# Moving the second half's combine behind the last expert, and the first w1 loads onto the ScalarE queue, in an eight-core recurrent + MoE layer

## Chip, cores and metric

The kernel runs on the 8 cores of one Trainium2 chip. Each core works on one of 8 sequences (2048 tokens of width 1024) and exchanges nothing with the others. The metric is the device time in microseconds of the slowest core.

## The reference, cut to what matters

```python
xn = _layernorm(x)
s  = _L0_attn_ref(xn, ...)               # recurrent attention
g  = _silu(_L0_ffn_ref(xn, ...))         # 8 routed experts + 1 shared
return x + s * g
# _L0_ffn_ref:
gates = sum(one_hot(top_k(softmax(x @ w_router.T), 2)) * vals)
acc = gelu(x @ Ws1.T + bs1) @ Ws2.T + bs2
acc = acc + sum_e gates_e * (gelu(x @ W1_e.T + b1_e) @ W2_e.T + b2_e)
return SCALE * acc
```

Every expert is computed for every token and weighted by its gate, which is zero for the experts that are not chosen.

## The kernel before

The program is recorded in Python as one list of instructions for each engine; each engine runs its list in order. The helper `op` derives semaphore waits from the last writer and the readers of whole tiles, so a read of one block of `acc` waits for the last write to any block of it. An engine's list holds its DMA issues too, and these wait in place: what stands behind a waiting DMA issue waits as well.

Stages, in order: the prologue normalises and transposes x; A and B compute the recurrent part; B2 computes `s` and writes it to DRAM as `s_scr` in 16 blocks of 128 tokens. Meanwhile GpSimd's queue casts all expert weights to bf16 copies in DRAM (`w1s`, `w2s`). A barrier ends each stage. The last stage, `ph_ffn`, is the subject here.

`ph_ffn` first loads router weights and biases (L861 to L866), then computes the gates of 16 token blocks, one after the other (L874 matmuls, L884 Exp on ScalarE, a chain of small VectorE operations, L914 transpose). Then it treats the tokens in two halves (`th` = 0, 1) of 1024. For each half it sets `acc` to the gated output biases (L970, L974) and goes through 9 experts. Of each expert:

- phase 1 (L995): 512 matmuls of 128x128 by 128x512 make the hidden layer, with `w1s` coming in four 2 MB quarters into two buffers `w1b`; ScalarE applies Gelu (L1006). The first two quarters of the next expert are loaded ahead by ScalarE's queue (L1043); only the very first expert's are loaded at L984, quarter 0 by SyncE and quarter 1 by GpSimd, as quarters 2 and 3 are.
- phase 2 (L1027), in two parts `qq` of four token blocks: 256 matmuls each, with `w2s` in 256 KB pieces through a ring of six buffers, loaded alternately by SyncE and GpSimd (L1017). After each part VectorE adds the eight banks of PSUM to `acc` (L1053, or L1059 for the shared expert, which is the last of the nine).

Then the *combine*: for each of the half's 8 token blocks, load x and s, ScalarE's Tanh of `acc`, four VectorE operations, and the store of `out`. There is one `gfin` tile, and two each of `xres` and `sres`. For the first half this stands behind its last expert, with the DMAs on SyncE (L1075 to L1093): loads of a block, then its store, then the loads of the next. For the second half `mk_combine_t1` makes eight pieces of work with all DMAs on ScalarE's queue (L935 to L958); four are put into the list during part `qq` = 1 of the last expert, behind its matmul steps 4, 12, 20 and 28, and the other four are put behind everything. They may start early because blocks 0 to 3 of `acc` are final after part `qq` = 0.

Of the kernel before, what the change touches and what calls it, by code (L numbers as in the profile page):

```python
# [11 lines left out]
AF = mybir.ActivationFunctionType  # L12
ALU = mybir.AluOpType
# [14 lines left out]
NE = 9  # L28
EPS = 1e-5
SCALE = 1.0 / math.sqrt(1.25)  # L30
# [811 lines left out]
def ph_ffn(p, env):  # L842
    op, da, A16, A32 = p.op, env["da"], env["A16"], env["A32"]
# [3 lines left out]
    w1b = [A16.alloc((8, NC_, 128), f"w1b{j}") for j in range(2)]  # L847
# [8 lines left out]
    acc = A32.alloc((8, D), "acc")  # L856
    xres = [A32.alloc((D,), f"xres{j}") for j in range(2)]
    sres = [A32.alloc((D,), f"sres{j}") for j in range(2)]
    gfin = A32.alloc((D,), "gfin")

    op("gpsimd", lambda E: E.dma_start(  # L861
        out=wrt.ap(), in_=da["w_routert"].rearrange("(c p) m -> p c m", p=128)),
       writes=[wrt.buf])
    op("gpsimd", lambda E: E.dma_start(out=b2e[0:NE, :], in_=da["b2ext"][:, :]),
       writes=[b2e.buf])
    op("sync", lambda E: E.dma_start(  # L866
        out=b1t.ap().rearrange("p (a b) -> p a b", a=NE), in_=da["b1t"][:, :, :]),
       writes=[b1t.buf])

    for i in range(NT):  # L870
        t0 = i * 128
        bap, bbs = bankof(env, 2, 0)
        for c in range(NC_):
# [3 lines left out]
               reads=([xnT.buf, wrt.buf] if c in (0, NC_ - 1) else []),  # L877
               writes=bbs if c == NC_ - 1 else [],
               war=bbs if c == 0 else [], inc=(c == NC_ - 1))
        op("vector", lambda E, bap=bap: E.reduce_max(gtmp[:, 0:1], bap[:, 0:8], axis=AX.X),  # L880
           reads=bbs, writes=[gtmp.buf])
        op("vector", lambda E: E.tensor_scalar_mul(gtmp[:, 1:2], gtmp[:, 0:1], -1.0),
           reads=[gtmp.buf], writes=[gtmp.buf])
        op("scalar", lambda E, bap=bap, i=i: E.activation(  # L884
            gates[:, i, :], bap[:, 0:8], AF.Exp, bias=gtmp[:, 1:2]),
           reads=bbs + [gtmp.buf], writes=[gates.buf])
        op("vector", lambda E, i=i: E.reduce_sum(gtmp[:, 2:3], gates[:, i, :], axis=AX.X),
           reads=[gates.buf], writes=[gtmp.buf])
        op("vector", lambda E: E.reciprocal(gtmp[:, 3:4], gtmp[:, 2:3]),
           reads=[gtmp.buf], writes=[gtmp.buf])  # L890
        op("vector", lambda E, i=i: E.tensor_scalar(
            gates[:, i, :], gates[:, i, :], gtmp[:, 3:4], None, ALU.mult),
           reads=[gtmp.buf, gates.buf], writes=[gates.buf])
# [29 lines left out]
            in_=gates.ap().rearrange("p a b -> p (a b)")),  # L923
            reads=[gates.buf], dsem="b_dbg")

    pend = []

    def mk_combine_t1():
        its = []
        for tb in range(8):  # L930
            i = 8 + tb

            def it(tb=tb, i=i):
                xr, sr = xres[tb % 2], sres[tb % 2]
                op("scalar", lambda E, i=i, xr=xr: E.dma_start(  # L935
                    out=xr.ap(), in_=da["x"][i * 128:(i + 1) * 128, :]),
                   writes=[xr.buf], dsem="b_" + xr.buf.name + "_t1")
                op("scalar", lambda E, i=i, sr=sr: E.dma_start(
                    out=sr.ap(), in_=env["s_scr"][i * 128:(i + 1) * 128, :]),
                   reads=[env["s_scr_buf"]], writes=[sr.buf],  # L940
                   dsem="b_" + sr.buf.name + "_t1")
                op("scalar", lambda E, tb=tb: E.activation(
                    gfin.ap(), acc[:, tb, :], AF.Tanh, scale=SCALE / 2),
                   reads=[acc.buf], writes=[gfin.buf])
                op("vector", lambda E: E.tensor_scalar(
                    gfin.ap(), gfin.ap(), 0.5, 0.5, ALU.mult, ALU.add),
                   reads=[gfin.buf], writes=[gfin.buf])
                op("vector", lambda E, tb=tb: E.scalar_tensor_tensor(
                    gfin.ap(), acc[:, tb, :], SCALE, gfin.ap(), ALU.mult,
                    ALU.mult),  # L950
                   reads=[acc.buf, gfin.buf], writes=[gfin.buf])
                op("vector", lambda E, sr=sr: E.tensor_mul(
                    sr.ap(), sr.ap(), gfin.ap()),
                   reads=[sr.buf, gfin.buf], writes=[sr.buf])
                op("vector", lambda E, xr=xr, sr=sr: E.tensor_add(
                    sr.ap(), sr.ap(), xr.ap()),
                   reads=[xr.buf, sr.buf], writes=[sr.buf])
                op("scalar", lambda E, i=i, sr=sr: E.dma_start(  # L958
                    out=env["out"][i * 128:(i + 1) * 128, :], in_=sr.ap()),
                   reads=[sr.buf], dsem=f"b_out{2 + tb % 2}")  # L960
            its.append(it)
        return its

    for th in range(2):
        t0 = th * 1024
        for tb in range(8):
# [10 lines left out]
        for e in range(NE):  # L977
            idx = th * NE + e
            for q in range(4):
                wb = w1b[q % 2]  # L980
                if not (q < 2 and idx > 0):
                    qeng = "sync" if q % 2 == 0 else "gpsimd"
                    p.raw_wait(qeng, f"cast{e}", 32)
                    op(qeng, lambda E, e=e, q=q, wb=wb: E.dma_start(  # L984
                        out=wb.ap(), in_=env["w1s"][e, q * 8:(q + 1) * 8].rearrange(
                            "f (c p) m -> p f c m", p=128)),
                       writes=[wb.buf])
                for fi in range(8):
                    ffb = q * 8 + fi
                    banks = [bankof(env, (ffb % 2), tc) for tc in range(2)]  # L990
                    for c in range(NC_):
                        for tc in range(2):
                            bap, bbs = banks[tc]
                            op("tensor", lambda E, wb=wb, fi=fi, c=c, bap=bap,
                               tt=t0 + tc * 512: E.matmul(  # L995
                                bap, wb[:, fi, c, :], xnT[:, c, tt:tt + 512],
                                start=(c == 0), stop=(c == NC_ - 1)),
                               reads=([wb.buf, xnT.buf]
                                      if (c == 0 and tc == 0) or (c == NC_ - 1 and tc == 1)
                                      else []),  # L1000
                               writes=bbs if c == NC_ - 1 else [],
                               war=bbs if c == 0 else [],
                               inc=(c == NC_ - 1))
                    for tc in range(2):
                        bap, bbs = banks[tc]
                        op("scalar", lambda E, e=e, ffb=ffb, tc=tc, bap=bap: E.activation(  # L1006
                            Hsb[:, ffb, tc * 512:(tc + 1) * 512], bap,
                            AF.Gelu_apprx_tanh,
                            bias=b1t[:, e * 32 + ffb:e * 32 + ffb + 1]),
                           reads=bbs + [b1t.buf], writes=[Hsb.buf])  # L1010
            for qq in range(2):
                for ffc in range(32):
                    pc = qq * 32 + ffc
                    wb2 = w2b[pc % 6]
                    qeng = "sync" if pc % 2 == 0 else "gpsimd"
                    p.raw_wait(qeng, f"cast{e}", 32)
                    op(qeng, lambda E, e=e, ffc=ffc, wb2=wb2: E.dma_start(  # L1017
                        out=wb2.ap(), in_=env["w2s"][e, ffc * 128:(ffc + 1) * 128, :]
                        .rearrange("(f p) d -> p f d", p=128)),
                       writes=[wb2.buf])  # L1020
                    for tb in range(4):
                        tbg = qq * 4 + tb
                        for dh in range(2):
                            first = (tb == 0 and dh == 0)
                            last = (tb == 3 and dh == 1)
                            op("tensor", lambda E, wb2=wb2, tb=tb, dh=dh,
                               tbg=tbg, ffc=ffc: E.matmul(  # L1027
                                ps[tb][:, dh * 512:(dh + 1) * 512],
                                Hsb[:, ffc, tbg * 128:(tbg + 1) * 128],
                                wb2[:, 0, dh * 512:(dh + 1) * 512],  # L1030
                                start=(ffc == 0), stop=(ffc == 31)),
                               reads=([wb2.buf, Hsb.buf] if (first or last) else []),
                               writes=[psb[2 * tb + dh]] if ffc == 31 else [],
                               war=[psb[2 * tb + dh]] if ffc == 0 else [],
                               inc=(ffc == 31 or last))
                    if pend and ffc in (4, 12, 20, 28):
                        pend.pop(0)()
                if qq == 0 and idx + 1 < 2 * NE:
                    th2, e2 = divmod(idx + 1, NE)
                    for q2, peng in ((0, "scalar"), (1, "scalar")):  # L1040
# [6 lines left out]
                for tb in range(4):  # L1047
                    tbg = qq * 4 + tb
                    ti = th * 8 + tbg
                    for dh in range(2):  # L1050
# [7 lines left out]
                        else:  # L1058
# [1 line left out]
                                acc[:, tbg, sl], acc[:, tbg, sl], ps[tb][:, sl]),  # L1060
                               reads=[psb[2 * tb + dh], acc.buf],
                               writes=[acc.buf])
                if th == 1 and e == NE - 1:
                    cmb = mk_combine_t1() if qq == 0 else cmb
                    pend.extend(cmb[0:4] if qq == 0 else cmb[4:8])
        accname = f"acc{th}"
        if accname in env["dbg"]:
            p.op("sync", lambda E, accname=accname: E.dma_start(
                out=env["dbg"][accname][:, :],
                in_=acc.ap().rearrange("p a b -> p (a b)")),  # L1070
                reads=[acc.buf], dsem="b_dbg")
        for tb in range(8 if th == 0 else 0):
            i = th * 8 + tb
            xr, sr = xres[tb % 2], sres[tb % 2]
            op("sync", lambda E, i=i, xr=xr: E.dma_start(  # L1075
# [17 lines left out]
            op("sync", lambda E, i=i, sr=sr: E.dma_start(  # L1093
                out=env["out"][i * 128:(i + 1) * 128, :], in_=sr.ap()),
               reads=[sr.buf], dsem=f"b_out{tb % 2}")
    while pend:
        pend.pop(0)()
    for bo in ("b_out0", "b_out1", "b_out2", "b_out3"):
        p.raw_wait("sync", bo, p.cnt.get(bo, 0))


# [14 lines left out]
```

How the kernel before makes its waits and increments, by code:

```python
        def run(E, wl=wl, fn=fn, inc=inc, csem=csem, amt=amt):  # L165
            for sem, v in wl:
                E.wait_ge(sems[sem], v)
            ins = fn(E)
            if inc:
                ins.then_inc(sems[csem], amt)
# [2 lines left out]
    def raw_wait(self, eng, sem, val):  # L173
        if val <= 0:
            return
        wd = self.waited[eng]
        if sem != eng and wd.get(sem, -1) >= val:
            return
        if sem != eng:
            wd[sem] = val
        sems = self.sems
        self.prog[eng].append(lambda E: E.wait_ge(sems[sem], val))
# [218 lines left out]
        def c1(E, e=e):  # L401
            E.dma_start(out=env["w1s"][e], in_=env["da"]["w1p"][e]).then_inc(
                sems[f"cast{e}"], 16)
        def c2(E, e=e):
            E.dma_start(out=env["w2s"][e], in_=env["da"]["w2p"][e]).then_inc(
                sems[f"cast{e}"], 16)
```

## Time and profile before

| what | us |
|---|---|
| timed runs (2) | 7484.86 and 7590.48, median 7537.67 |
| profiled execution, its own time | 6895.18 |
| its span, slowest core (core 5) | 6893.6 |
| spans of the eight cores | 6850.7 to 6893.6 |

The profiled execution is 642.5 us shorter than the median of the timed runs. All durations of single instructions are of the profiled execution, on core 5.

### The profile page before, as it was taken

To read this page: it belongs to the slowest core of one execution; us is meant where nothing else is said; L and a number is where in the kernel's file an instruction comes from. 1 tells how busy PE (TensorE), PEld (TensorE's weight loads), DVE (VectorE), ACT (ScalarE), POOL (GpSimd) and SP (SyncE) were. 2 spreads that over 40 slices of the span, in tenths; PEclk is the share of its full clock that TensorE was granted. 3 is DMA by queue.
4 is the path that set the end of the run, shared out by engine and by line. 5 is a ranking of instruction groups with operands and counts; after the bars stand their busy time and mean duration, and the time that the engine had idled before them with its cause. 6 is when DMAs were issued, how large, how long until landed. Compare 5 with 4: busy or idle time off the path is not lost.

```text
span 6893.6 us, 65364 instructions; the slowest of 8 cores (6850.7 to 6893.6 us)
## 1 busy us (share of the span) xinstructions
PE 4878.0 (71%) x21024; PEld 2113.4 (31%) x21024; DVE 1357.3 (20%) x4215; ACT 1216.2 (18%) x2432; POOL 381.9 (6%) x630
## 2 busy tenths in 40 slices
PE   2353222221042439999999999995999999999997
PEld 0111010110011114444444444442444444444443
DVE  4454444443232340000000000002000000000002
ACT  1001222223400002211221121121122112211220
POOL 0000000000000000001000100000100010001000
PEclk9865555555565659999999999997999999999998
DMA  1106999802999513344334433443433443344335
GB/s 43 25 0 77 110 110 110 95 0 36 109 116 116 80 35 93 87 129 118 101 93 119 126 101 96 113 124 113 130 95 86 130 123 101 87 130 123 100 88 162
DMA packets 274970, 660.29 MB, mean 96 GB/s; under 512 B 25063, under 2 KB 136103, under 8 KB 270000
## 3 DMA queue, kind: packets, MB, share of 16 engines
q0 software_dynamic: 69776, 351.68, 31.2%
q1 hardware_dynamic: 131232, 220.55, 11.4%
q10 hardware_dynamic: 73632, 83.89, 5.0%
q8 instruction: 179, 2.93, 0.2%
q14 instruction: 151, 1.24, 0.1%
HBM read 800.05 MB, written 167.77 MB: 140 GB/s over the span
## 4 chain that ended last, share of the span: by engine, by line
PE 63%; DVE 15%; issue 7%; DMA 7%; ACT 4%; another core or an unknown queue 3%; DVEq 1%; ACTq 0%; SPq 0%; POOLq 0%
PE ps L995 29%; PE ps L1027 25%; DMA arena<-w2s 3%; DMA s_scr<-arena 2%; DVE arena L437 2%; DVE arena L1053 2%; PE ps L605 1%; ACT arena L671 1%; PE ps L451 1%; DVEq L167 1%; PE ps L387 1%; PE ps L820 1%; PE ps L677 1%; PE ps L790 1%
## 5 line engine op out<-in xcount | busy, mean ns | idle before, releaser
L1027 PE MATMUL ps<-arena 128*128 128x512 bf16 x9216 | 2059.2, 384 | 109.7 <-DVE arena L1053 46.3
L995 PE MATMUL ps<-arena 128*128 128x512 bf16 x9216 | 1999.4, 380 | 3.2 <-DVE arena L1053 3.2
L1006 ACT ACTIVATE arena<-ps,arena 128x512 bf16<-128x512 f32 x1152 | 791.5, 687 | 3146.6 <-PE ps L995 3091.3
L1027 PEld LDWEIGHTS ps<-arena 128*128 128x128 bf16 x9216 | 906.6, 99 | 1262.3 <-issue 226.2
L995 PEld LDWEIGHTS ps<-arena 128*128 128x128 bf16 x9216 | 901.5, 98 | 1098.4 <-issue 17.9
L1053 DVE SCALAR_TENSOR_TENSOR arena<-ps,arena 128x512 f32<-128x512 f32 x256 | 192.1, 750 | 3524.0 <-PE ps L1027 3500.3
L433 PE MATMUL ps<-arena 32*128 32x128 bf16 (+1 forms) x352 | 107.4, 326 | 550.9 <-DVE arena L437 467.5
L1017 POOL DMA_DIRECT2D arena<-w2s x576 | 309.4, 538 | 2625.8 <-PE ps L1027 2535.2
L677 PE MATMUL ps<-arena 128*32 128x32 bf16 (+3 forms) x256 | 51.8, 202 | 405.5 <-DVE arena L674 405.5
L433 PEld LDWEIGHTS ps<-arena 32*128 32x128 bf16 x352 | 31.5, 98 | 631.0 <-issue 631.0
L387 PE MATMUL ps<-arena 128*128 128x128 f32 x128 | 57.1, 446 | 198.0 <-DVE arena L383 130.2
L437 DVE SCALAR_TENSOR_TENSOR arena<-ps,arena 128x128 bf16<-128x128 f32 (+1 forms) x352 | 160.3, 455 | 82.4 <-PE ps L433 78.8
L677 PEld LDWEIGHTS ps<-arena 128*32 128x32 bf16 (+3 forms) x256 | 31.1, 122 | 424.7 <-issue 424.7
L984 POOL DMA_DIRECT2D arena<-w1s x19 | 52.7, 2772 | 1355.1 <-PE ps L995 1201.0
L671 ACT ACTIVATE arena<-arena 128x32 bf16<-128x32 f32 (+3 forms) x256 | 92.4, 361 | 195.7 <-DVE arena L667 195.7
L812 PE MATMUL ps<-arena 128*128 128x128 f32 x128 | 51.6, 403 | 105.7 <-DVE arena L815 67.8
L796 ACT ACTIVATE arena<-ps 128x512 bf16<-128x512 f32 x32 | 19.1, 597 | 585.5 <-PE ps L790 585.4
L643 PE MATMUL ps<-arena 128*128 128x256 bf16 x64 | 22.4, 350 | 139.4 <-DVE arena L646 139.4
L605 PE MATMUL ps<-arena 128*128 128x512 bf16 x256 | 96.4, 559 | 28.1 <-DVE arena L441 19.1
L441 DVE TENSOR_TENSOR arena<-arena 128x128 bf16<-128x128 bf16 (+1 forms) x352 | 98.5, 280 | 37.0 <-DVE arena L437 0.5
L820 PE MATMUL ps<-arena 128*128 128x512 bf16 x256 | 97.4, 563 | 9.9 <-DVE arena L815 9.9
L790 PE MATMUL ps<-arena 128*128 128x512 bf16 x256 | 89.1, 525 | 21.0 <-DVE arena L800 12.3
(143 smaller groups left out, 1821.9 us busy)
## 6 DMA issues: line engine op xcount, KB each, us to landing
arena<-w2s SPq DMA_DIRECT2D x576, 256.0 KB, 3.1
arena<-w2s POOLq DMA_DIRECT2D x576, 256.0 KB, 3.0
w1s<-w1p POOLq DMA_DIRECT2D x9, 8192.0 KB, 402.2
w2s<-w2p POOLq DMA_DIRECT2D x9, 8192.0 KB, 480.1
arena<-w1s POOLq DMA_DIRECT2D x19, 2048.0 KB, 14.8
arena<-x SPq DMA_DIRECT2D x24, 512.0 KB, 3.6
s_scr<-arena SPq DMA_DIRECT2D x16, 512.0 KB, 46.4
arena<-s_scr SPq DMA_DIRECT2D x8, 512.0 KB, 5.4
```

The lines of the kernel that those rows point to most:

```text
L433: op("tensor", lambda E, c=c, bap=bap, zrow=zrow, slot=slot, t0=t0, w=width: E.matmul(bap[:, 0:w], env["w_x2s"][0:32, slot, c * 128:(c + 1 ...
L437: op("vector", lambda E, c=c, bap=bap, slot=slot, w=width, mb=mb: E.scalar_tensor_tensor(mb[:, 0:w], bap[:, 0:w], xbias[:, slot * NC_ + c: ...
L605: op("tensor", lambda E, vh=vh, c=c, bap=bap: E.matmul(bap, xmixB[:, c, :], w_vt[:, c, vh * 512:(vh + 1) * 512], start=(c == 0), stop=(c = ...
L671: op("scalar", lambda E, sw=sw, mid=mid, eq=eq, NB=NB, nng=nng: E.activation(eq[:, 0:sw], NB(0, sw), AF.Exp, bias=nng[:, mid:mid + 1]), re ...
L677: op("tensor", lambda E, sw=sw, pm_ap=pm_ap, kb=kb, qb=qb: E.matmul(pm_ap[0:sw, :], kb[:, 0:sw], qb[:, 0:CSUB], start=True, stop=True), re ...
L790: op("tensor", lambda E, vh=vh, c=c, bap=bap: E.matmul(bap, xmixB[:, c, :], w_gt[:, c, vh * 512:(vh + 1) * 512], start=(c == 0), stop=(c = ...
L820: op("tensor", lambda E, oh=oh, c=c, bap=bap, ogTj=ogTj: E.matmul(bap, ogTj[:, c, :], w_ot[:, c, oh * 512:(oh + 1) * 512], start=(c == 0), ...
L995: tt=t0 + tc * 512: E.matmul(bap, wb[:, fi, c, :], xnT[:, c, tt:tt + 512], start=(c == 0), stop=(c == NC_ - 1)),
L1006: op("scalar", lambda E, e=e, ffb=ffb, tc=tc, bap=bap: E.activation(Hsb[:, ffb, tc * 512:(tc + 1) * 512], bap, AF.Gelu_apprx_tanh, bias=b1 ...
L1017: op(qeng, lambda E, e=e, ffc=ffc, wb2=wb2: E.dma_start(out=wb2.ap(), in_=env["w2s"][e, ffc * 128:(ffc + 1) * 128, :] .rearrange("(f p) d ...
L1027: tbg=tbg, ffc=ffc: E.matmul(ps[tb][:, dh * 512:(dh + 1) * 512], Hsb[:, ffc, tbg * 128:(tbg + 1) * 128], wb2[:, 0, dh * 512:(dh + 1) * 512 ...
L1053: op("vector", lambda E, tb=tb, tbg=tbg, ti=ti, e=e, sl=sl: E.scalar_tensor_tensor(acc[:, tbg, sl], ps[tb][:, sl], gates[:, ti, e:e + 1], ...
```

## The change

Two edits. (1) The loads of the first expert's w1 quarters 0 and 1 move from SyncE's and GpSimd's lists to ScalarE's, ahead of the router. (2) `mk_combine_t1` and its interleaving go; both halves use the same loop, behind the half's last expert, with the DMAs on SyncE.

```diff
+    for q0 in range(2):
+        wb = w1b[q0]
+        p.raw_wait("scalar", "cast0", 32)
+        op("scalar", lambda E, q0=q0, wb=wb: E.dma_start(
+            out=wb.ap(), in_=env["w1s"][0, q0 * 8:(q0 + 1) * 8]
+            .rearrange("f (c p) m -> p f c m", p=128)),
+           writes=[wb.buf], dsem="b_" + wb.buf.name + "_pf")
...
-    def mk_combine_t1():
...
-                if not (q < 2 and idx > 0):
+                if q >= 2:
                     qeng = "sync" if q % 2 == 0 else "gpsimd"
...
-                    if pend and ffc in (4, 12, 20, 28):
-                        pend.pop(0)()
...
-                if th == 1 and e == NE - 1:
-                    cmb = mk_combine_t1() if qq == 0 else cmb
-                    pend.extend(cmb[0:4] if qq == 0 else cmb[4:8])
...
-        for tb in range(8 if th == 0 else 0):
+        for tb in range(8):
...
-    while pend:
-        pend.pop(0)()
-    for bo in ("b_out0", "b_out1", "b_out2", "b_out3"):
-        p.raw_wait("sync", bo, p.cnt.get(bo, 0))
+    p.raw_wait("sync", "b_out0", p.cnt.get("b_out0", 0))
+    p.raw_wait("sync", "b_out1", p.cnt.get("b_out1", 0))
```

**VectorE, last expert of the second half.** Before, between the additions of part 0 (first row, L1059 x8) and those of part 1 stand four combines of four operations each, of which the first is shown; `arena` is the on-chip memory.

```order
L1059 TENSOR_TENSOR arena<-arena,ps 128x512 x8
L945 TENSOR_SCALAR arena<-arena 128x1024
L948 SCALAR_TENSOR_TENSOR arena<-arena 128x1024
L952 TENSOR_TENSOR arena<-arena 128x1024
L955 TENSOR_TENSOR arena<-arena 128x1024
```

After, both parts' additions (L1026 x16) stand together and all eight combines behind them:

```order
L1020 SCALAR_TENSOR_TENSOR arena<-ps,arena 128x512 x128
L1026 TENSOR_TENSOR arena<-arena,ps 128x512 x16
L1047 TENSOR_SCALAR arena<-arena 128x1024
L1050 SCALAR_TENSOR_TENSOR arena<-arena 128x1024
L1053 TENSOR_TENSOR arena<-arena 128x1024
L1055 TENSOR_TENSOR arena<-arena 128x1024
```

Four combines moved from beside the matmuls of part 1 to behind them.

**The queue that carries the combine's DMAs, end of the program.** Before, it is ScalarE's, behind the last Gelu:

```order
L1006 ACTIVATE arena<-ps,arena 128x512 x64
L935 DMA arena<-x 128x1024
L938 DMA arena<-s_scr 128x1024
L942 ACTIVATE arena<-arena 128x1024
L958 DMA out<-arena 128x1024
```

After, it is SyncE's, behind the last w2 loads (L986):

```order
L953 DMA arena<-w1s 128x64x128
L986 DMA arena<-w2s 128x1024 x32
L1039 DMA arena<-x 128x1024
L1041 DMA arena<-s_scr 128x1024
L1057 DMA out<-arena 128x1024
```

In both, the loads of the next block stand behind the store of this one, and the store waits for this block's last VectorE operation.

**ScalarE, start of the last stage.** After, two w1 loads stand ahead of the router's Exp (L891, before L884):

```order
L796 ACTIVATE arena<-ps 128x512 x32
L872 DMA arena<-w1s 128x64x128 x2
L891 ACTIVATE arena<-ps,arena 128x8 x16
L975 ACTIVATE arena<-ps,arena 128x512 x64
L1010 DMA arena<-w1s 128x64x128 x2
```

Before, L796 was followed by the Exp at once, and SyncE and GpSimd had one such load more each.

## Rows read from the trace of the kernel before

**Rows 1.** The page: span, and part 1 (busy us, share of the span)

```profile
span 6893.6 us, 65364 instructions; the slowest of 8 cores (6850.7 to 6893.6 us)
...
PE 4878.0 (71%) x21024; PEld 2113.4 (31%) x21024; DVE 1357.3 (20%) x4215; ACT 1216.2 (18%) x2432; POOL 381.9 (6%) x630
```

**Rows 2.** Busy by stretch: length, PE, PEld, DVE, ACT, POOL, clock, DMA, GB/s

```profile
2597.60:6852.50 4254.90, 4064.75 (x18449) 1809.70 (x18448) 273.60 (x348) 809.08 (x1199) 359.09 (x594) 0.98 0.41 111
0.00:2498.10 2498.10, 794.92 (x2416) 294.92 (x2416) 1012.93 (x3607) 397.32 (x1212) 18.60 (x33) 0.62 0.60 72
```

**Rows 3.** TensorE's waits, 2597 to 6852 us: total, times, longest

```profile
PE ps L970 <- DVE arena L974: 74.3, 15, 71.3
...
PE ps L1027 <- DMA arena<-w2s: 30.2, 27, 4.8
```

**Rows 4.** Timeline of the program's end (start us, length us)

```profile
6851.05 6.23 DVE L1059 TENSOR_TENSOR arena<-arena,ps 128x512 f32<-128x512 f32 x8 [16.19 <-PE ps L1027]
...
6863.29 0.34 ACTq L958 DMA_DIRECT2D out<-arena  x1
...
6890.70 0.34 ACTq L958 DMA_DIRECT2D out<-arena  x1
```

**Rows 5.** A group of instructions, 6851 to 6893.6 us: busy us, mean ns, idle before

```profile
L945 DVE TENSOR_SCALAR arena<-arena 128x1024 f32<-128x1024 f32 x4 | 2.8, 694 | 10.2 <-ACT arena L942 10.2
```

**Rows 6.** Timeline of the first half's combine

```profile
4684.97 6.23 DVE L1059 TENSOR_TENSOR arena<-arena,ps 128x512 f32<-128x512 f32 x8 [53.84 <-PE ps L1027]
...
4697.22 0.34 SPq L1093 DMA_DIRECT2D out<-arena  x1
...
4703.67 1.22 DVE L1089 TENSOR_TENSOR arena<-arena 128x1024 f32<-128x1024 f32 x1 [4.58 <-DMA arena<-s_scr]
...
4760.74 0.34 SPq L1093 DMA_DIRECT2D out<-arena  x1
```

**Rows 7.** The first half's loads of s (line L1077): issues and landing

```profile
L1077 SPq DMA_DIRECT2D arena<-s_scr x8: 663/674/720, 4675.1 to 4752.6; - x8
...
DMA to landing us min/median/max: 5.2/5.4/7.1
```

**Rows 8.** TensorE's timeline in part 1 of three experts, the last one in three pieces

```profile
4948.95 56.60 PE L1027 MATMUL ps<-arena 128*128 128x512 bf16 x249 [0.27 <-DVE arena L1053]
...
5416.31 55.04 PE L1027 MATMUL ps<-arena 128*128 128x512 bf16 x249 [0.27 <-DVE arena L1053]
...
6796.90 15.92 PE L1027 MATMUL ps<-arena 128*128 128x512 bf16 x73 [0.41 <-DVE arena L1059]
...
6813.90 31.26 PE L1027 MATMUL ps<-arena 128*128 128x512 bf16 x144 [1.08 <-DMA arena<-w2s]
...
6845.39 7.07 PE L1027 MATMUL ps<-arena 128*128 128x512 bf16 x32 [0.23 <-DMA arena<-w2s]
```

**Rows 9.** Waits of all engines, 6792 to 6853 us: total, times, longest

```profile
POOL arena L1017 <- issue: 5.0, 1, 5.0
...
PE ps L1027 <- DMA arena<-w2s: 1.3, 2, 1.1
```

**Rows 10.** Timeline of the last stage's start

```profile
2498.61 0.91 POOL L861 DMA_DIRECT2D arena<-w_routert  x1 [811.46 <-DMA s_scr<-arena]
...
2506.69 1.28 ACT L884 ACT_TABLE_LOAD   x1 [31.47 <-DVE arena L882]
...
2597.60 42.58 PE L995 MATMUL ps<-arena 128*128 128x512 bf16 x185
```

**Rows 11.** DMA issues, 2498 to 2530 us (count, KB, us to landing)

```profile
arena<-w_routert POOLq DMA_DIRECT2D x1, 16.0 KB, 7.0
...
arena<-w1s SPq DMA_DIRECT2D x1, 0.2 KB, 22.5
```

**Rows 12.** Timeline of ScalarE's queue, the second w1 load of the first pair

```profile
2712.79 9.62 ACTq L1043 DMA_DIRECT2D arena<-w1s  x1
```

**Rows 13.** Line L1043, all 34 issues: ns min/median/max

```profile
L1043 ACTq DMA_DIRECT2D arena<-w1s x34: 681/4596/12419, 2711.7 to 6505.6; - x34
```

More of the change, by code:

```diff
@@ L924, in ph_ffn @@
             reads=[gates.buf], dsem="b_dbg")
-    pend = []
-    def mk_combine_t1():
[L929 to L962, printed above, removed]
     for th in range(2):
```

## The prediction

> **What bounds the kernel now.** I first read busy time by engine: TensorE is busy 4878 us of a span of 6893.6 [rows 1]. An average over stages with different limits says little of a change in one place, so I next read it by stretch. From 2597.6 to 6852.5 us, the experts, TensorE is busy 4065 of 4255 us at a granted clock of 0.98 of the full 2.4 GHz; in the 2498 us before it is busy 795, so chains between engines set the pace there [rows 2]. The change touches nothing of those chains. Third, TensorE's waits among the experts: the longest, 71.3 us, is for VectorE between the halves; it is the first half's combine, which the next half's bias matmuls stand behind [rows 3]. All waits for w2 pieces make 30.2 us in 27 cases [rows 3]. Last I read the timeline at the end, since the change is there: behind the last additions come four combines, then the program is over [rows 4]. Nothing lies beside those; every microsecond there is span.
>
> **The tail, before.** The last additions start at 6851.05 and the last store is issued at 6890.70: 39.65 us for eight additions and four blocks [rows 4]. A block takes (6890.70 - 6863.29) / 3 = 9.14 us. VectorE's four operations are only 0.69 + 3 x 1.22 = 4.36 us of that [rows 5, 6]; the rest is the queue's order: store, then the next block's loads, then VectorE waits for s.
>
> **The tail, after.** All eight blocks stand behind the additions. The first half's combine is exactly that already: same eight blocks, same loop, same queue. It runs from the additions at 4684.97 to the eighth store at 4760.74, 75.77 us; its blocks take (4760.74 - 4697.22) / 7 = 9.07 us, with VectorE waiting 4.58 us for s in one [rows 6]. The first block's loads were issued at about 4675.1, ahead of the additions, behind the last w2 load, and landed in 7.1 us at most [rows 7], so they were hidden; they will be again. The tail grows by 75.77 - 39.65 = 36.1 us. What lies behind the last store, its landing, is there in both.
>
> The Tanh of block 0 reads `acc` as a whole. So it waits for the last addition even though blocks 0 to 3 are final much earlier, and the DMA issues behind the first store on SyncE wait with it. Nothing of TensorE stands behind them: the program ends there. The bounds of this term: if the loads ran ahead and only VectorE set the pace, eight blocks would take 8 x (4.36 + about 0.4 of gaps) = 38 us and the tail 6.3 + 38 + 1.2 = 46 us, +6; if s took the 7.1 us seen once instead of 5.4 [rows 7] in each of seven blocks, +36 + 12 = +48. I take +36, since the first half is the same code.
>
> **What goes from beside the matmuls.** Four combines with their loads and stores ran beside part 1 of the last expert. Did they slow it? Its 249 ungated matmuls took 15.92 + 1.08 + 31.26 + 0.23 + 7.07 = 55.56 us [rows 8]. In other experts' part 1, with no combine beside, the same 249 took 55.04 to 56.60 [rows 8], so no loss shows. The waits in this stretch put 1.3 us on w2 pieces [rows 9], which is the most I can give back by waits. Going back to the others' worst would cost 1.0. Range -1.3 to +1.0; I take 0. Here the Trainium skill (SBUF — State Buffer, section "Who interferes with whom") speaks for more: VectorE operations with two on-chip inputs or in the two-port mode hold a port pair that GpSimd needs, so GpSimd's descriptors for w2 could starve behind the sixteen combine operations, 4 x 4.36 = 17.5 us of them. The trace agrees in kind, with one 5.0 us gap on GpSimd that no other engine explains [rows 9], but the six-buffer ring swallowed all but 1.3 us; by the rule at full price the change would give back 5 us, and the sum would be lower by 5.
>
> **The w1 loads at the start.** In the old order they were issued at about 2498.6 and 2500 us and the slower landed 22.5 us after [rows 11], at 2521. TensorE starts on them at 2597.60 with no wait for a transfer [rows 10]. So 76 us of cover were there, made by the router; an earlier or later issue of a few microseconds earns nothing: 0. But ScalarE's list now holds two large issues ahead of its first Exp, and the second of such a pair does not return at once: in the first expert it held ScalarE for 9.62 us [rows 12], and over all 34 issues, half of which are second ones, they run from 0.68 to 12.42 us [rows 13]. My reading is that the second waits until the first has drained in part. The first would be issued at about 2498.6 and take 0.7; the second then ends at 2499.4 + 9.6 = 2509.0, or at 2511.8 with the longest. ScalarE's first work there, a table load, started at 2506.69 [rows 10], and the router's chain waits for it. So the router starts 2509.0 - 2506.7 = 2.3 us later; the bounds are 0 (a second issue of under 7 us, since no w2 load competes here) and +5.1. I take +2.
>
> What can be late too is the router's own weights: issued at 2498.61, landed in 7.0 us beside one SyncE load of the same size [rows 10, 11]. Bounds: at best a few microseconds sooner, since GpSimd's own w1 load is gone, and at worst behind the whole of such a load, 22.5 instead of 7.0, +15.5. I take 0, by the nearest row, since a 2 MB load already ran beside it. The Trainium skill (DMA: Bandwidth & Descriptors, section "Queues, rings and completion order") says that each DMA engine takes packets from its queues in turn, which speaks against the full +15.5; the 7.0 us beside a 22.5 us load agrees.
>
> GpSimd's and SyncE's lists lose one issue each; what follows them, w1 quarters 2 and 3, waits for TensorE anyway. Quarter 2 now also follows another semaphore for the same buffer, long satisfied. 0.
>
> **Sum.** Tail 36.1, matmuls 0, ScalarE's late start 2, the rest 0: +38 us on the profiled execution, so 6895.2 becomes 6933. The timed runs lie 642.5 us above the profiled one, a factor of 1.093, and I cannot say from these rows in which stage. The tail is VectorE and DMA; if it stretched with the rest, +42, if not, +38. I predict 7537.7 + 40 = 7578 us, 0.5% slower. A measurement of this kernel tells about 2% from no change (151 us), and its own two runs differ by 106 us, so the verdict should be "no change".
>
> **Rivals.**
> (a) *The loads of the tail run ahead*, so that the SyncE's queue, free of Tanh, keeps up with VectorE: tail 46 us, +6, with the late start +8, about 7546. Together with the give-back of the w2 waits (1.3 to 5 us) and a router that starts on time, this ends at 0 or just above: not slower. For it: two buffers each of x and s. Against: the first half has the same queue and the same buffers, and waits 4.58 us in a block. 5%.
> (b) *The router starves behind the w1 loads*: +15.5 in place of the 2, total +52, about 7590. 8%. Still within 2%.
> (c) *Slower by more than 2%*: the place is the eight-block tail on all eight cores at once; the s loads would have to meet a jam. The price: over 113 us beyond the +38, so 16 us and more for each of seven loads, against 5.4 in the median and 7.1 at most [rows 7]. Against it: eight cores went through the first half's combine at about the same time at 5.4. I give the mechanism 1%. To it comes that a run may fall in a stretch of lower clock on the expert matmuls: the profiled run and the timed ones differ by 9.3%, both of one kernel, and a clock 2% lower over 4255 us is 85 us.
> (d) *The interleaving did harm*, and the matmuls beside it gain: at most the 5 us above. 3%; total +33, 7571.
> (e) *The change does not do what it says*: the order shows all eight combines behind the sixteen additions. 0.
>
> **Numbers.** The forecast, +34 to +45, has 80%, (a) 5, (b) 8, (d) 3, (c) 1, other 3. All but (c) lie from 0 to +52, so their spread is small; the spread of the timed runs, 0.7% to either side of the median (53 us), is larger and sets the range: 7546 - 53 = 7493 to 7590 + 53 = 7643, rounded outward to 7490 and 7655. For the three verdicts: slower by over 2% needs 111 us of drift on top of 40, faster needs 191. From runs 106 us apart I give 0.07 and 0.03, and 0.9 to within 2%.
>
> **What would show it.** Right: behind the last additions eight stores, the last about 76 us after the additions' start, 9.1 us apart, each with VectorE waiting about 4.6 us for s; part 1 of the last expert in 55 to 56.6 us for 249 matmuls; no wait for w1 at the first expert; router weights landed in about 7 us; ScalarE's second early w1 issue lasting 7 to 12 us and its first Exp 0 to 5 us later than it was. Wrong: blocks 5 us apart (rival a), 7 us much exceeded at the router (b), or w2 waits in other experts that changed, which nothing here explains.

## The result, and the profile after

| | before | after |
|---|---|---|
| timed runs, median (us) | 7434.86 (11 runs, 6887.39 to 7694.42) | 6937.34 (12 runs, 6928.07 to 7744.96) |
| ratio of the undisturbed runs | | 1.0061, 95% interval 1.0046 to 1.0077 |
| profiled execution, its own time (us) | 6895.18 | 6929.01 |
| spans of the cores (us) | 6850.7 to 6893.6 | 6905.9 to 6927.5 |

The medians cannot be compared: in many executions of either kernel, and in all 65 of any kernel here that took over 7000 us and have their clocks on record, the cores of one die or both show a lower granted TensorE clock (0.73 to 0.82 instead of 0.84 in the mean) and take some per cent longer, and the ratio leaves these out. By the ratio the change costs 0.61% of about 6890 us, that is 42 us (32 to 53), less than the 2% that would count as a verdict of slower.

The page of the changed kernel, answering to [rows 1]:

```profile
span 6927.5 us, 65369 instructions; the slowest of 8 cores (6905.9 to 6927.5 us)
## 1 busy us (share of the span) xinstructions
PE 4868.3 (70%) x21024; PEld 2110.9 (30%) x21024; DVE 1356.9 (20%) x4215; ACT 1218.9 (18%) x2434; POOL 379.3 (5%) x629
```

No engine's busy time moved by more than 10 us: the same work, put elsewhere. The end of the program, from the timeline of core 4, the slowest (answering to [rows 4, 6]; start, length, idle before and who ended it):

```profile
6835.59 0.37 SPq L1039 DMA_DIRECT2D arena<-x  x1
6836.06 0.52 SPq L1041 DMA_DIRECT2D arena<-s_scr  x1
6845.84 6.23 DVE L1026 TENSOR_TENSOR arena<-arena,ps 128x512 f32<-128x512 f32 x8 [54.40 <-PE ps L996]
...
6858.08 0.34 SPq L1057 DMA_DIRECT2D out<-arena  x1
...
6866.09 1.23 DVE L1053 TENSOR_TENSOR arena<-arena 128x1024 f32<-128x1024 f32 x1 [6.13 <-DMA arena<-s_scr]
...
6903.51 1.23 DVE L1053 TENSOR_TENSOR arena<-arena 128x1024 f32<-128x1024 f32 x1 [4.59 <-DMA arena<-s_scr]
...
6924.58 0.34 SPq L1057 DMA_DIRECT2D out<-arena  x1
```

The loads of the first block are issued ten microseconds ahead of the additions, as forecast, and cost nothing. From the additions to the eighth store it takes 78.74 us here, against 39.65 [rows 4]. In the mean of the eight cores it is 76.8 us against 39.8: +37.0. VectorE's wait for s is 4.6 to 4.8 us in five of the seven later blocks here, 6.13 in the second and 5.26 in the third.

The other place is the start of the last stage, answering to [rows 10]:

```profile
2498.34 0.80 ACTq L872 DMA_DIRECT2D arena<-w1s  x1
2498.72 0.91 POOL L861 DMA_DIRECT2D arena<-w_routert  x1 [810.27 <-DMA s_scr<-arena]
...
2499.60 11.38 ACTq L872 DMA_DIRECT2D arena<-w1s  x1
...
2512.54 0.36 PE L881 MATMUL ps<-arena 128*128 128x8 bf16 x8 [20.32 <-DMA arena<-w_routert]
...
2513.51 1.28 ACT L891 ACT_TABLE_LOAD   x1 [13.93 <-DVE arena L889]
```

The router's weights, issued at 2498.72, landed only 13.7 us later, where they took 7.0 [rows 11]. TensorE waited 20.32 us in front of the router; over the cores it is 18.3 us against 13.9, later on every core, by 1.8 to 7.2 us and by 4.4 in the mean. ScalarE's second issue lasts 11.38 us and ends at 2510.98, before the weights have landed. So it is not what the first Exp waited for; it ends 0.5 to 3.4 us before the table load on every core.

37.0 + 4.4 = 41.4 us, and the ratio says 42. The mean of the eight spans grew by 41.5 us, from 6872.0 to 6913.5. The two terms account for it. What they are made of was tried in eight kernels. For single microseconds the timing is too coarse; there the rows of all eight cores are compared.

### The profile page after: what moved, and what is told of

Read it like the earlier page. It is cut to its first block, busy times and chain, and to the rows that moved or that the text cites. A ratio compares the mean times of both kernels' runs of the same rounds, so it can differ in the third digit from the quotient of the medians.

```text
span 6927.5 us, 65369 instructions; the slowest of 8 cores (6905.9 to 6927.5 us)
## 1 busy us (share of the span) xinstructions
PE 4868.3 (70%) x21024; PEld 2110.9 (30%) x21024; DVE 1356.9 (20%) x4215; ACT 1218.9 (18%) x2434; POOL 379.3 (5%) x629
## 3 DMA queue, kind: packets, MB, share of 16 engines
q1 hardware_dynamic: 132624, 231.04, 11.7%
## 4 chain that ended last, share of the span: by engine, by line
PE 63%; DVE 15%; DMA 7%; issue 7%; ACT 4%; another core or an unknown queue 3%; DVEq 1%; ACTq 0%; SPq 0%; POOLq 0%
PE ps L964 29%; PE ps L996 25%; DMA arena<-w2s 3%; DMA s_scr<-arena 2%; DVE arena L437 2%; DVE arena L1020 2%; PE ps L605 1%; ACT arena L671 1%; DMA arena<-s_scr 1%; PE ps L451 1%; DVEq L167 1%; PE ps L387 1%; PE ps L820 1%; PE ps L677 1%
## 5 line engine op out<-in xcount | busy, mean ns | idle before, releaser
L996 PE MATMUL ps<-arena 128*128 128x512 bf16 x9216 | 2056.8, 384 | 100.6 <-DVE arena L1020 46.8
L964 PE MATMUL ps<-arena 128*128 128x512 bf16 x9216 | 1997.7, 379 | 3.2 <-DVE arena L1020 3.2
L986 POOL DMA_DIRECT2D arena<-w2s x576 | 309.6, 538 | 2614.6 <-PE ps L996 2511.3
L796 ACT ACTIVATE arena<-ps 128x512 bf16<-128x512 f32 x32 | 19.1, 597 | 585.5 <-PE ps L790 585.4
L605 PE MATMUL ps<-arena 128*128 128x512 bf16 x256 | 96.3, 558 | 28.1 <-DVE arena L441 19.2
L1026 DVE TENSOR_TENSOR arena<-arena,ps 128x512 f32<-128x512 f32 x32 | 22.0, 687 | 436.0 <-PE ps L996 432.7
L820 PE MATMUL ps<-arena 128*128 128x512 bf16 x256 | 96.6, 560 | 9.9 <-DVE arena L815 9.9
```

The lines of the kernel that those rows point to most:

```text
L605: op("tensor", lambda E, vh=vh, c=c, bap=bap: E.matmul(bap, xmixB[:, c, :], w_vt[:, c, vh * 512:(vh + 1) * 512], start=(c == 0), stop=(c = ...
L820: op("tensor", lambda E, oh=oh, c=c, bap=bap, ogTj=ogTj: E.matmul(bap, ogTj[:, c, :], w_ot[:, c, oh * 512:(oh + 1) * 512], start=(c == 0), ...
L964: tt=t0 + tc * 512: E.matmul(bap, wb[:, fi, c, :], xnT[:, c, tt:tt + 512], start=(c == 0), stop=(c == NC_ - 1)),
L986: op(qeng, lambda E, e=e, ffc=ffc, wb2=wb2: E.dma_start(out=wb2.ap(), in_=env["w2s"][e, ffc * 128:(ffc + 1) * 128, :] .rearrange("(f p) d ...
L996: tbg=tbg, ffc=ffc: E.matmul(ps[tb][:, dh * 512:(dh + 1) * 512], Hsb[:, ffc, tbg * 128:(tbg + 1) * 128], wb2[:, 0, dh * 512:(dh + 1) * 512 ...
```

## Experiments

**1. Each edit alone.** `tail_only` undoes the first edit:

```diff
-    for q0 in range(2):
-        wb = w1b[q0]
-        p.raw_wait("scalar", "cast0", 32)
...
-                if q >= 2:
+                if not (q < 2 and idx > 0):
```

> The changed kernel with its first edit undone: the first expert's w1 quarters are loaded by SyncE and GpSimd again, the second half's combine stands behind the last expert. Theory (two terms: 37 us of exposed combine in the tail, and about 4.4 us because the router's weights land later): the tail from the last additions to the last store stays 76 to 78 us on every core, TensorE's wait for the router's weights goes back from 18.3 us in the mean of the cores to about 14, and the time is 37 us over before (ratio 1.0054). Rival (the w1 loads are free, the tail is everything): the wait stays at 18, ratio as with both edits.

`pf_only` is the kernel before with that edit alone.

> The kernel before with the first edit alone: both w1 quarters from ScalarE's queue, ahead of the router. Theory: the router's weights land in 10 to 13.7 us instead of 7, TensorE's wait for them is 18 us instead of 14 in the mean of the cores, tail 39.8 us as before, ratio 1.0006, which timing cannot tell from 1. Rival (ScalarE's second issue is what holds the router, by 2 to 5 us): the weights land in 7 us and the first Exp starts only when that issue ends.

Means over the eight cores (us):

| | before | after | tail_only | pf_only |
|---|---|---|---|---|
| last additions to last store | 39.8 | 76.8 | 77.8 | 40.9 |
| router's weights, issue to landing | 7.2 | 11.8 | 8.2 | 11.3 |
| TensorE's wait in front of the router | 13.9 | 18.3 | 14.5 | 17.5 |
| ratio to before (interval) | | 1.0061 (1.0046 to 1.0077) | 1.0049 (1.0012 to 1.0086) | 0.9979 (0.9923 to 1.0034) |

The edits part cleanly: the tail follows the second, the router's wait the first. The rival that the w1 loads are free falls by the rows; the timing of `pf_only`, some 14 us below before where 4 above were expected, has an interval that holds both 0 and +4. Its tail is 1.1 us longer than before's, by longer waits for s on three cores; no run gives a reason for them. In `tail_only` three cores landed the weights in 9.9 to 11.3 us all the same, so the old order does not rule the long landing out, it makes it rarer (4 of 16 core readings of the old order are 9.9 us or more, one of them in the kernel before; all 24 with a w1 load ahead are, counting the next run).

**2. One load or two ahead of the router's weights?** `one_pf` leaves only quarter 0 on ScalarE's queue:

```diff
-    for q0 in range(2):
+    for q0 in range(1):
...
-                if q >= 2:
+                if q >= 2 or (q == 1 and idx == 0):
```

> The changed kernel with only quarter 0 of the first expert's w1 on ScalarE's queue; quarter 1 goes back to GpSimd, behind the router's weights. Theory A (a 2 MB load issued some tenths of a us ahead of the router's weights is in their way): they still land in 10 us or more. Theory B (it takes the two loads in a row to be in their way, or ScalarE being held): they land in 7 us and the wait is 14. Tail 76 to 78 us in both; ratio 1.005 to 1.006.

Core 4, the slowest:

```profile
2497.17 0.80 ACTq L872 DMA_DIRECT2D arena<-w1s  x1
2497.55 0.91 POOL L861 DMA_DIRECT2D arena<-w_routert  x1 [813.84 <-DMA s_scr<-arena]
...
2512.42 0.35 PE L881 MATMUL ps<-arena 128*128 128x8 bf16 x8 [21.60 <-DMA arena<-w_routert]
```

The weights landed in 9.9 to 14.7 us, 11.8 in the mean, and TensorE waited 18.2. Theory A holds: one 2 MB load is enough. Issued 0.38 us ahead of the weights it is in their way. Issued 0.03 to 0.07 us behind, as SyncE does it in the old order, it mostly is not (12 of 16 core readings). The transfers' packets show the same order: in `before` and `tail_only` the router's first packet starts before any of w1 on all 16 cores, and in the changed kernel, `pf_only` and `one_pf` 86 to 786 packets of w1, of 1 KB each, start before it on all 24. One thing is not separated: the load ahead is on ScalarE's queue and the one behind on SyncE's, and no run has the same queue in both orders. The ratio was 1.0045 (0.9995 to 1.0095).

**3. No load ahead.** `rt_first` puts the pair behind the first router block's Exp, on the same queue:

```diff
+        if i == 0:
+            for q0 in range(2):
+                wb = w1b[q0]
+                p.raw_wait("scalar", "cast0", 32)
...
```

> The changed kernel with the two w1 loads of ScalarE's queue put behind the first router block's Exp. Theory: with no w1 load under way the router's weights land in under 7 us, so the first router block starts some 5 to 8 us earlier than in the changed kernel; but ScalarE's second issue then runs 8 to 12 us and the Exp of block 1 starts late by some 5 us, which gives most of it back. Rival (the landing time is the queue's own and has nothing to do with the w1 loads): it stays at 10 us or more. Tail 76 to 78 us, ratio about 1.006.

Core 1, the slowest:

```profile
2500.70 0.91 POOL L861 DMA_DIRECT2D arena<-w_routert  x1 [813.43 <-DMA s_scr<-arena]
2503.72 0.36 PE L874 MATMUL ps<-arena 128*128 128x8 bf16 x8 [9.31 <-DMA arena<-w_routert]
...
2505.98 0.27 ACT L884 ACTIVATE arena<-ps,arena 128x8 f32<-128x8 f32 x1
2505.99 9.85 ACTq L891 DMA_DIRECT2D arena<-w1s  x1
...
2516.00 0.27 ACT L884 ACTIVATE arena<-ps,arena 128x8 f32<-128x8 f32 x1 [9.75 <-issue]
```

With no w1 load under way the weights land in 2.8 to 3.0 us on all cores, so even the 7 us of the kernel before were mostly the w1 load beside them. And the second issue holds ScalarE: block 1's Exp waits 9.75 us for "issue", an instruction of its own list, and starts at 2516.00 instead of some 5 us sooner. From the weights' issue to the last bias matmul it takes 98.9 us in the mean against 103.2 in the changed kernel: of the 8.9 us won at the landing, 4.6 were given back. Both halves came out as expected, the first a little above its 5 to 8 us. Ratio 1.0031 (0.9982 to 1.008).

**4. ScalarE's hold without its cover.** `wrt_early` is the changed kernel with the router's weights loaded in the stage before; the later load goes:

```diff
+    wrt = A16.alloc((NC_, 8), "wrt")
+    env["wrt"] = wrt
+    op("gpsimd", lambda E: E.dma_start(
+        out=wrt.ap(), in_=da["w_routert"].rearrange("(c p) m -> p c m", p=128)),
+       writes=[wrt.buf])
     op("gpsimd", lambda E: E.dma_start(
         out=w_gt.ap(), in_=da["w_gt"]...
...
-    wrt = A16.alloc((NC_, 8), "wrt")
+    wrt = env["wrt"]
...
-    op("gpsimd", lambda E: E.dma_start(
-        out=wrt.ap(), in_=da["w_routert"].rearrange("(c p) m -> p c m", p=128)),
-       writes=[wrt.buf])
```

> The changed kernel with the router's weights loaded a stage earlier, ahead of GpSimd's last casts; the w1 loads stay on ScalarE's queue. Theory (the late landing of the router's weights costs 4.4 us and the landing as such 10 or more): TensorE's wait in front of the router, 18.3 us, falls to 6 to 9. What is late next is ScalarE: its second w1 issue lasts 9 to 11 us from the barrier, so the first Exp cannot start before; so the router gains only some 3 us over the changed kernel, not 10. Rival (ScalarE's hold costs nothing since it falls in another wait): it gains the whole 10. Tail as in the changed kernel, ratio 1.004 to 1.006.

```profile
2490.21 0.35 PE L883 MATMUL ps<-arena 128*128 128x8 bf16 x8 [6.27 <-DMA s_scr<-arena]
2490.25 0.81 ACTq L874 DMA_DIRECT2D arena<-w1s  x1
...
2491.38 9.86 ACTq L874 DMA_DIRECT2D arena<-w1s  x1
2501.38 1.28 ACT L893 ACT_TABLE_LOAD   x1 [10.04 <-issue]
```

TensorE starts the router at once after the barrier, with 5.8 to 6.3 us of waiting that is the barrier's own, and then the result lies there until ScalarE's issue returns. Counted from SyncE's first issue behind the barrier, and in the mean of the cores, the table load starts after 10.9 us here, after 13.3 in the changed kernel and after 8.8 in the one before. The first expert's matmuls start 101.9 us after that point here, 104.3 in the changed kernel and 99.8 in the one before. So the router gains 2.4 us over the changed kernel, not 10: the rival falls, and ScalarE's hold alone costs 2.1 us against before. The term of the prediction is real, but only once the weights are not later still. The profiled execution took 6915.4 us, against 6876 to 6883 for the kernel before on the same chip (the executions that a ratio counts).

**5. What sets the pace of a block in the tail.** `tail_ahead` issues the loads of block tb+1 ahead of the store of block tb, in both halves (`ld` is the pair of loads):

```diff
+        ld(0)
         for tb in range(8):
             i = th * 8 + tb
             xr, sr = xres[tb % 2], sres[tb % 2]
-            op("sync", lambda E, i=i, xr=xr: E.dma_start(...
+            if tb < 7:
+                ld(tb + 1)
```

> The changed kernel with one thing more: in both halves' combine the loads of block tb+1 stand ahead of the store of block tb on SyncE's queue. Theory (the queue's order, store and then loads, sets the 9.1 us of a block, of which VectorE works 4.4): a block then takes about 5.9 us, set by the s load that waits for the store two blocks back (3 us to land, 5.6 us for the load, two VectorE operations, over two blocks); the tail falls from 76.8 to about 54 us and the gap between the halves shrinks by as much, so the time is 45 us under the changed kernel and level with before or just under (ratio about 1.000). Rival (VectorE, or the transfers' own time with all eight cores at it, sets the pace): blocks stay above 8 us and the ratio at 1.005.

```profile
6834.58 0.34 SPq L1063 DMA_DIRECT2D out<-arena  x1
...
6838.65 0.32 SPq L1041 DMA_DIRECT2D arena<-s_scr  x1
...
6839.55 0.34 SPq L1063 DMA_DIRECT2D out<-arena  x1
...
6843.78 1.23 DVE L1059 TENSOR_TENSOR arena<-arena 128x1024 f32<-128x1024 f32 x1 [2.36 <-DMA arena<-s_scr]
...
6848.89 1.23 DVE L1059 TENSOR_TENSOR arena<-arena 128x1024 f32<-128x1024 f32 x1 [0.61 <-DMA arena<-s_scr]
```

From the additions to VectorE's last operation it takes 53.0 us in the mean against 76.7 in the changed kernel; TensorE's wait between the halves fell from 72.5 to 47.5 us in the mean of the cores. Together that is 49 us, against the 42 that the change had cost. Ratio 1.0002 (0.9976 to 1.0028). What a block waits for now: the load of s at 6838.65 goes into the buffer that the store of 6834.58 reads, and is issued only 4.1 us after it, when that has landed; so four blocks take 24 us on core 4, 6.0 each, and not VectorE's 4.4.

**6. What holds blocks 0 to 3 back.** `acc_split` gives each of the eight blocks of `acc` its own dependency in the changed kernel:

```diff
     acc = A32.alloc((8, D), "acc")
+    accb = [Buf(f"acc{j}") for j in range(8)]
...
-               reads=[acc.buf], writes=[gfin.buf])
+               reads=[accb[tb]], writes=[gfin.buf])
```

> The changed kernel with a dependency of its own for each of the eight blocks of acc, nothing else. The prediction said that blocks 0 to 3 wait because the Tanh reads acc as a whole. If that holds them, the combines of four blocks slip beside the last matmuls and the tail falls from 76.8 by up to 36 us. If the order of VectorE's own list holds them (both parts' additions stand ahead of the first combine), only the first Tanh starts early and the tail loses 1.3 us: 75.5.

The tail took 74.4 us in the mean against 76.8, not 40. The reason that the prediction gave falls: what holds the blocks is the place of the combines in VectorE's list, behind the additions. Where most of the 2.4 us come from, core 4's timeline shows:

```profile
6813.67 5.65 DVE L1027 TENSOR_TENSOR arena<-arena,ps 128x512 f32<-128x512 f32 x8 [54.33 <-PE ps L997]
6819.24 0.69 DVE L1048 TENSOR_SCALAR arena<-arena 128x1024 f32<-128x1024 f32 x1
```

The first combine operation starts with the end of the additions, with no wait for a Tanh (1.25 us in the changed kernel), and the additions no longer wait for one another: eight take 5.65 us where they took 6.23. Together it is 5.57 us from the additions to the first combine operation against 7.48. The same shows beyond the tail: TensorE's waits for the additions among the experts fell from 54.9 us to 40.4 on core 4. The profiled execution took 6894.9 us, against the 6876 to 6883 for the kernel before on that chip: by this one execution the finer dependencies gave back more than half of the 42 us, and mostly outside the tail.

**7. A version that beats both.** `best1` keeps before's interleaving and adds what the runs above taught: loads ahead of stores, router weights a stage earlier, first w1 loads on SyncE and GpSimd; and it takes the first half's combine with the second half's bias sums out of the gap between the halves:

```diff
+                    if th == 1 and e == 0 and ffb % 3 == 1 and ffb // 3 < 8:
+                        ccomb("sync", 0, ffb // 3)
+                        accinit(1, ffb // 3)
```

> A version meant to beat both: before's interleaving of four blocks; in the tail the other four with loads ahead; the first half's combine and the second half's bias sums moved among the matmuls of the next expert's phase 1, one block every three steps; router weights loaded a stage earlier; first w1 loads on SyncE and GpSimd. Theory: the 84 us between the halves (71.3 us combine and 12.6 us bias sums) fall to under 5, the tail goes from 39.8 to about 31, TensorE's wait at the router from 14 to 6: about 95 to 100 us under before, ratio 0.986. Rival (the combine beside phase 1 starves the w1 loads or ScalarE's Gelu and stalls TensorE): the gap comes back as waits in that phase, which takes well over 113 us, and the ratio stays above 0.993.

The timeline of TensorE across the seam between the halves, core 3:

```profile
4663.32 7.30 PE L1009 MATMUL ps<-arena 128*128 128x512 bf16 x32
4670.56 0.60 PE L970 MATMUL ps<-arena 9*128 9x512 bf16 x2
4671.09 10.53 PE L1009 MATMUL ps<-arena 128*128 128x512 bf16 x48
4681.56 0.60 PE L970 MATMUL ps<-arena 9*128 9x512 bf16 x2
```

There is no gap left where 71.3 us were [rows 3]: two bias matmuls of 0.60 us together stand in front of each 48. All waits of TensorE from 4640 to 4860 us add up to 5.3 us, 1.6 of them for Gelu and none for w1, and the tail is 27.5 us long in the mean of the cores. Ratio 0.987 (0.9829 to 0.991), some 90 us under the kernel before; the rival, a stall of w1 or Gelu, is not seen. With neither the weights' landing nor ScalarE's hold in front of it, the first expert starts 92.6 us after the barrier, where it was 99.8 before and 101.9 in `wrt_early`: at its full price, with nothing to hide it, the hold costs 9.3 us. One thing went against it. The last expert's part 1, from the first to the second additions, took 62.5 us in the mean of the cores (58.9 to 68.8) instead of 60.5. On the core with 68.8 the row of that stretch reads

```profile
6700.00:6768.00 68.00, 64.66 (x254) 26.53 (x252) 22.25 (x24) 4.23 (x4) 7.53 (x14) 0.86 0.68 216
```

which is a granted clock of 0.86 with 0.8 us of waits for w2; in the kernel before, core 5 had 1.00 from 6796.9 to 6852.6 us, the same stretch of work. Whether the busier seam causes that was not tried and stays open.

## Why the prediction was right or wrong

**The tail: right.** +36.1 forecast from the first half's combine, +37.0 measured in the mean of the cores. The 0.9 us over it are waits for s a little above the 4.58 us of the row, 4.7 in the mean; only the slowest core has a block with 6.13. A block takes 9.2 us where 9.1 was forecast. The cause in the queue's order and the pattern of the waits came out; `tail_ahead` shows the cause. Its bound from below, 46 us with loads run ahead, was too low for two buffers: 53.

**Why blocks 0 to 3 wait: wrong.** "The Tanh of block 0 reads acc as a whole. So it waits for the last addition" named a lesser cause; the order of VectorE's list is the one that binds (`acc_split`: 74.4 us where 40 would have shown the other). The number did not depend on it.

**The matmuls beside the combine: right.** 0 forecast. From the first to the second additions of the last expert it is 60.5 us before and 60.0 after in the mean of the cores. The gain by the Trainium skill's rule on the shared port (SBUF — State Buffer, "Who interferes with whom") does not appear: 5 us were its full price, 0.6 are seen, and `tail_only`, which has no combine there either, has 60.6. The page is narrower than the prediction had it: an operation with two on-chip inputs contends with those operations of GpSimd alone that read on-chip memory, and the full block is the two-port mode's, which by the page leaves at most the 4 TENSOR_SCALAR operations of the 16.

**The start of the stage: too low, and for the wrong reason.** +2 was forecast, for ScalarE's hold, and 0 for the router's weights with an upper bound of +15.5. Measured: +4.4 for the weights and nothing more for the hold, which ends first; with the weights there in time the hold costs 2.1 (`wrt_early`), as sized. The step that failed is "I take 0, by the nearest row, since a 2 MB load already ran beside it". The row had a load issued 0.03 us *behind* the weights; the change issues one 0.38 us *ahead*, and `one_pf` shows that a single such load makes the weights land in 11.8 us instead of 7.2. Rival (b) had the right mechanism with 8%, at less than its price, +4.4 and not +15.5. The Trainium skill's rule that each DMA engine takes packets from its queues in turn (DMA: Bandwidth & Descriptors, "Queues, rings and completion order") fits in so far as the weights landed before the load did; but they take 3 us alone, 7 beside and 12 behind it, and with a load ahead 1.5 to 2.2 MB of w1 had started by the router's last packet, so sharing is not free.

**The absolute time: wrong, and this made the forecast miss.** The sum on the profiled execution came out: 6933 forecast, 6929.0 measured. Part of that is luck. Both terms were low, the tail by 0.9 us and the start by 2.4, and the two profiled executions differ by only 33.8 us where their cores differ by 41.5 in the mean, because the slowest core of the first stood further above its mean. The step that failed is the one after the sum: "The timed runs lie 642.5 us above the profiled one ... I predict 7537.7 + 40 = 7578 us". I took a distance that I could not explain for a property of the kernel and built the range, 7490 to 7655, around it. The runs show no such distance: the median of the changed kernel is 6937.34, 8.3 us above its profiled execution. The kernel before was itself timed again with the change, and three of those executions took 6887 to 6896 us. The likely cause of the 642.5 us is the lower granted clock told with the result; for the two runs behind the 7537.67 us no clock is on record, so for them it is not shown. The sign lay open, since the same program had also run in 6895 us. Rival (c) even named a lower clock, but only as a way to be slower. A range that leaned on the profiled time would have held; the ratio, 1.0053 forecast against 1.0061, did.

## What to carry to other kernels

A queue's list that holds a block's store ahead of the next block's loads makes the transfer's latency part of every block; find it by a wait for the load that repeats, and swap the two before moving work elsewhere. A large prefetch had two prices here that its landing time does not show: it delayed a small load that was issued just behind it, and the second of two in a row held the engine that issued it. Where two times of the same kernel differ by more than the kernel can explain, do not carry the distance into a forecast: forecast the change, and give it as a ratio.

## What the runs showed that was not expected

- The landing time of a 16 KB load with 1024 rows of 16 bytes: 2.8 to 3.0 us alone (`rt_first`), 6.2 to 7.1 in 7 of 8 cores beside a 2 MB load issued 0.03 to 0.07 us behind it (before), 9.9 to 14.7 behind one issued 0.38 us ahead (`after`, `pf_only`, `one_pf`, all 24 readings).
- A second 2 MB issue from ScalarE holds that engine for 8.4 to 11.7 us at the start of the stage, in all 48 core readings of six kernels, though only small loads compete; in the 17 pairs among the experts of the kernel before it is 8.4 to 12.4 us on core 5, and the first of a pair takes 0.7 to 0.8.
- Moving 84 us of combine and bias sums under matmuls costs TensorE only its own 4.8 us of bias matmuls: at a granted clock of 1.00 in the 117 us from 4663, TensorE was busy for 116.3 (`best1`).
